# A decoder layer on one core: the order of the steps on VectorE, GpSimd and ScalarE is rewritten

## What is computed

```
# mixer
zxbcdt = u @ W_in;  z, xBC, dt = split(zxbcdt);  dt = softplus(dt + dt_bias)
xBC = silu(conv4(xBC) + conv_b);  x, Bm, Cm = split(xBC)
y = ssd(x * dt, -exp(A_log) * dt, Bm, Cm, chunk=64) + x * D_param
yf = y * silu(z);  out = (yf * rsqrt(mean(yf*yf) + 1e-5) * norm_w) @ W_out
# cross-attention
q = rmsnorm(h @ Wq + bq) * qn_w;  k = rmsnorm(ctx @ Wk + bk) * kn_w;  v = ctx @ Wv + bv
out = softmax(q @ k.T * 128**-0.5 + mask) @ v @ Wo
# feed-forward, qa = 8-bit rounding per token, qw = weights rounded to -1, 0, 1 times a scale
h = silu(qa(x) @ qw(w_gate).T) * (qa(x) @ qw(w_up).T)
out = qa(rmsnorm(h) * ln_weight) @ qw(w_down).T
# layer
x = x + mixer(layernorm(x));  x = x + xattn(layernorm(x), ctx);  x = x + ffn(layernorm(x))
```

## Time and profile before

| | |
|---|---|
| device time, median of 3 runs | 1235.27 us (1234.82 to 1237.11) |
| the profiled execution's own time | 1235.27 us |
| its span in the trace | 1233.2 us |
| PE busy | 1152.9 us, 93% |
| PEld busy | 991.5 us, 80% |
| DVE busy | 1004.4 us, 81% |
| POOL busy | 960.3 us, 78% |
| ACT busy | 735.7 us, 60% |
| DMA, mean over the span | 30 GB/s |
| mean granted TensorE clock | 0.973 |

### The profile page before, as it was taken

One profiled execution on the slowest core, in us unless ns is written; L12 is line 12 of the kernel. 1 busy time (PEld: TensorE's weight loads), 2 busy tenths in 40 slices (PEclk: granted clock), 3 DMA queues, 4 the chain that ended last, 5 costly groups with the idle time before them and its releaser, 6 DMA issues.

```text
span 1233.2 us, 34450 instructions
## 1 busy us (share of the span) xinstructions
PE 1152.9 (93%) x11539; PEld 991.5 (80%) x11571; DVE 1004.4 (81%) x2508; ACT 735.7 (60%) x1878; POOL 960.3 (78%) x1532
## 2 busy tenths in 40 slices
PE   3787999999999999999999999999999999999863
PEld 3676888988888889888888898888888888887742
DVE  3676888888898888888888888898888888988654
ACT  3665666555566765566666655566665556666521
POOL 3687888988888888888888888888889888877641
PEclk8798999999999999999999999999999999999977
DMA  8310011000000000000000000000000000011000
GB/s 282 88 48 10 6 28 28 26 26 21 21 8 26 26 26 26 21 26 18 12 26 26 26 26 21 26 13 17 26 26 26 26 21 25 6 23 23 14 13 26
DMA packets 64455, 37.04 MB, mean 30 GB/s; under 512 B 41504, under 2 KB 62752, under 8 KB 64160
## 3 DMA queue, kind: packets, MB, share of 16 engines
q1 hardware_dynamic: 61488, 36.50, 10.5%
q10 hardware_dynamic: 2928, 0.03, 0.1%
HBM read 23.93 MB, written 4.19 MB: 23 GB/s over the span
## 4 chain that ended last, share of the span: by engine, by line
PE 56%; DVE 17%; issue 11%; POOL 9%; ACT 4%; DMA 2%; DVEq 0%; POOLq 0%; ACTq 0%; SPq 0%
PE bank L1428 14%; PE bank L1319 5%; PE bank L1320 5%; PE bank L1321 5%; PE bank L1347 4%; PE bank L1488 4%; PE bank L1401 3%; PE bank L1356 3%; DVE xc L959 3%; PE bank L1336 2%; PE bank L1551 2%; PE bank L1510 2%; DVE hh L1116 2%; PE bank L1544 1%; DVE yT L1009 1%
## 5 line engine op out<-in xcount | busy, mean ns | idle before, releaser
L1428 PE MATMUL bank<-xcT,wq 128*128 128x128 f32 x2048 | 236.0, 276 | 1.6 <-ACT xcT L712 1.6
L1428 PEld LDWEIGHTS bank<-xcT,wq 128*128 128x128 f32 x2048 | 231.1, 192 | 5.9 <-issue 2.0
L959 DVE SCALAR_TENSOR_TENSOR xc<-bank,cw,xc 128x124 f32<-128x124 f32 (+2 forms) x576 | 163.5, 339 | 13.8 <-ACT xc L682 9.0
L456 POOL TENSOR_TENSOR rq<-rq,minus_half 128x16 f32<-128x16 f32 x32 | 93.9, 2934 | 91.8 <-DVE rq L1060 91.8
L1319 PE MATMUL bank<-wo_hi,o_hi 128*128 128x256 f32 x512 | 149.5, 292 | 0.0
L1320 PE MATMUL bank<-wo_lo,o_hi 128*128 128x256 f32 x512 | 144.0, 281 | 0.0
L1321 PE MATMUL bank<-wo_hi,o_lo 128*128 128x256 f32 x512 | 143.8, 281 | 0.0
L731 ACT ACTIVATE qT<-bank,bqT 128x128 f32<-128x128 f32 x384 | 109.9, 369 | 54.5 <-PE bank L1428 54.3
L468 POOL TENSOR_TENSOR pr<-pr,mask 128x512 f32<-128x512 f32 x64 | 80.0, 1271 | 24.4 <-DVE pr L1067 24.3
L1319 PEld LDWEIGHTS bank<-wo_hi,o_hi 128*128 128x128 f32 x512 | 97.0, 189 | 0.5 <-issue 0.4
L1320 PEld LDWEIGHTS bank<-wo_lo,o_hi 128*128 128x128 f32 x512 | 96.9, 189 | 0.1
(11 more groups left out here) (231 smaller groups left out, 3396.6 us busy)
## 6 DMA issues: line engine op xcount, KB each, us to landing
x_in<-in_x SPq DMA_DIRECT2D x32, 128.0 KB, 2.1
c_in<-in_ctx SPq DMA_DIRECT2D x32, 128.0 KB, 2.0
x_m<-in_x SPq DMA_DIRECT2D x32, 128.0 KB, 2.2
out<-x SPq DMA_DIRECT2D x32, 128.0 KB, 1.7
wq<-in_L_xattn_Wq SPq DMA_DIRECT2D x1, 2048.0 KB, 14.4
stage<-in_L_xattn_Wo SPq DMA_DIRECT2D x2, 1024.0 KB, 7.4
w_in<-in_L_attn_W_in SPq DMA_DIRECT2D x1, 1024.0 KB, 6.1
qT<-in_L_ffn_w_gate SPq DMA_DIRECT2D x1, 1024.0 KB, 10.2
```

The lines of the kernel that those rows point to most:

```text
L456: g.tensor_tensor(rq[:, 1, :], rq[:, 0, :], minus_half[:, :], ALU.pow).then_inc(s["x_rq"].sem, 1)
L959: last = v.scalar_tensor_tensor(out=o, in0=src, scalar=cw[:, j, TAPS - 1 - back:TAPS - back], in1=o, op0=ALU.mult, op1=ALU.add)
L1428: last = mm(x_Qbank[g][:, (n % 4) * P:(n % 4 + 1) * P], wq[:, c, n * HD:(n + 1) * HD], xcT[:, c, :], start=(c == 0), stop=(c == DC - 1))
```

## The change

No instruction is added or taken away in the steady bodies, and PE's order and SP's order stay as they are. Steps trade places in `body` on three engines:

- POOL: `m_norm` goes from before `m_skip` to behind the first `x_o_low`; `x_split` is followed by the first `x_o_low`, and `f_scales` stands behind `m_norm`; `x_khat` goes ahead of `x_rms` and `m_rms`.
- ACT: `x_q_bias(2)` goes ahead of `m_tanh_x`; the second `x_o_copy` ahead of `f_T_copy`; two of the `x_o_high` copies trade places; `f_keep` goes behind `m_tanh_bc`.
- DVE: `m_weights` goes to the front, `m_average` behind `f_range`, `m_xdt` ahead of `m_mix`, `m_norm` behind `m_gate`, one `x_o_low` ahead of `m_gate` and the other between the two feed-forward halves, `x_q_mean` behind `m_total`, and in the tail of the body the order is `f_weight`, `m_conv_bc`, `f_highest`, `m_residual`, `m_silu_z`, `x_vb_add`. `f_value` is merged into `f_gate`, with the same two instructions.

The diff, cut:

```diff
@@ POOL body
-                if ms is not None and first not in (0, 1):
-                    m_norm(ms)
                 if m is not None:
                     m_skip(m)
...
                 if xa is not None and first != 1:
                     x_split(xa)
+                if xb is not None:
+                    x_o_low(xb, 0)
...
-                if first in (0, 1):
+                if ms is not None:
                     m_norm(ms)
                 if f is not None:
                     f_scales(f)
                 if xb is not None:
-                    x_o_low(xb, 0)
                     x_o_low(xb, 1)
...
                 if xa is not None:
+                    x_khat(xa)
                     x_rms(xa)
                 if m is not None and first not in (0, 1):
                     m_rms(m)
-                if xa is not None:
-                    x_khat(xa)
@@ ACT body
                     x_exp(xb, 1)
+                if xa is not None:
+                    x_q_bias(xa, 2)
                 if m is not None:
                     m_tanh_x(m)
                 if xa is not None:
-                    x_q_bias(xa, 2)
                     x_q_bias(xa, 3)
...
                     x_o_high(xb, 1, 1)
-                    x_o_high(xb, 0, 1)
+                    x_o_high(xb, 1, 0)
+                    x_o_copy(xb, 1)
                 if f is not None:
                     f_T_copy(f)
@@ DVE body
+                if m is not None:
+                    m_weights(m)
                 if ms is not None and first not in (-1, 0, 1):
                     m_spread(ms)
...
                 if m is not None:
+                    m_xdt(m)
                     m_mix(m)
-                    m_xdt(m)
                 if f is not None:
                     f_quant(f)
...
-                if ms is not None and first not in (-1, 0, 1):
-                    m_norm(ms)
                 if m is not None:
                     m_skip(m)
...
+                if xb is not None:
+                    x_o_low(xb, 1, 0)
                 if m is not None:
                     m_gate(m)
...
+                if ms is not None and first != 0:
                     m_norm(ms)
...
+                if xa is not None:
+                    x_kv(xa)
+                if f is not None:
+                    f_gate(f, 0)
                 if xb is not None:
                     x_o_low(xb, 0, 1)
...
                 if f is not None:
                     f_gate(f, 1)
-                if xa is not None:
-                    x_q_mean(xa)
-                if f is not None:
-                    f_value(f, 1)
...
                 if f is not None:
                     f_weight(f)
+                if mn is not None:
+                    m_conv_bc(mn)
+                if f is not None:
+                    f_highest(f)
```

More of the change, by code:

```diff
@@ L217, in decoder_layer @@
           x_sum0+x_inv0+x_sum1+x_inv1 x_p0+x_p1 x_PT0+x_PT1 x_pT0+x_pT1 x_O0+x_O1
[L218 removed]
+          x_oh00+x_of00+x_oh11+x_oh10+x_of11+x_oh01 x_ol00+x_ol11 x_ol10+x_ol01 x_out x_x2
           f_copy f_stats+f_mean f_veps+f_rstd f_xn f_am+f_am2+f_r+f_s f_q1+f_q2 f_T f_qTc
@@ L829, in body @@
                     x_o_high(xb, 1, 1)
-                    x_o_high(xb, 0, 1)
+                    x_o_high(xb, 1, 0)
+                    x_o_copy(xb, 1)
                 if f is not None:
                     f_T_copy(f)
-                if xb is not None:
-                    x_o_copy(xb, 1)
                 if xa is not None:
@@ L844, in body @@
                 if xb is not None:
-                    x_o_high(xb, 1, 0)
+                    x_o_high(xb, 0, 1)
                 if xa is not None or m is not None:
@@ L864, in body @@
                     f_square(f)
-                    f_keep(f)
                 if mn is not None:
@@ L877, in body @@
                     w_turned(2)
+                if f is not None:
+                    f_keep(f)
                 if first == 1:
@@ L1177, in body @@
                 if xb is not None:
+                    x_max(xb, 0)
                     x_max(xb, 1)
@@ L1187, in body @@
                     f_residual(fb)
-                if ms is not None and first not in (-1, 0, 1):
-                    m_average(ms)
                 if m is not None:
-                    m_weights(m)
                     m_silu_x(m)
@@ L1195, in body @@
                     f_range(f)
+                if ms is not None and first not in (-1, 0, 1):
+                    m_average(ms)
                 if m is not None:
+                    m_xdt(m)
                     m_mix(m)
-                    m_xdt(m)
                 if f is not None:
@@ L1204, in body @@
                     m_spread(ms)
-                if first == -1:
-                    m_average(ms)
-                    m_norm(ms)
-                if ms is not None and first not in (-1, 0, 1):
-                    m_norm(ms)
                 if m is not None:
@@ L1213, in body @@
                     dve.wait_ge(s["p_olo"].sem, 2)
+                if xb is not None:
+                    x_o_low(xb, 1, 0)
                 if m is not None:
                     m_gate(m)
-                if first in (0, 1):
+                if first in (-1, 0, 1):
                     m_average(ms)
@@ L1222, in body @@
                     w_round(1)
+                if ms is not None and first != 0:
                     m_norm(ms)
+                if first == 1:
                     dve.wait_ge(s["w_attn"].sem, 16 * W_ATTN)
-                if xb is not None:
-                    x_o_low(xb, 0, 1)
                 if xa is not None:
@@ L1230, in body @@
                     f_gate(f, 0)
-                    f_value(f, 0)
                 if xb is not None:
-                    x_o_low(xb, 1, 0)
+                    x_o_low(xb, 0, 1)
                 if f is not None:
                     f_gate(f, 1)
-                if xa is not None:
-                    x_q_mean(xa)
-                if f is not None:
-                    f_value(f, 1)
                 if first == 0:
@@ L1250, in body @@
                     m_total(m)
+                if xa is not None:
+                    x_q_mean(xa)
                 if first == -1:
@@ L1254, in body @@
                     m_dt_ratio(mn)
-                if xa is not None:
-                    x_vb_add(xa)
                 if f is not None:
                     f_weight(f)
+                if mn is not None:
+                    m_conv_bc(mn)
+                if f is not None:
+                    f_highest(f)
                 if first == 0:
                     x_norm(m)
+                if first in (-1, 0, 1):
+                    m_silu_bc(mn)
                 if m is not None and first != 0:
@@ L1263, in body @@
                     x_stats(m)
-                if f is not None:
-                    f_highest(f)
-                if mn is not None and first not in (-1, 0, 1):
+                if mn is not None:
                     m_silu_z(mn)
[L1268 to L1272, removed]
+                if xa is not None:
+                    x_vb_add(xa)
                 if f is not None:
@@ L1276, in body @@
                     x_residual(xb)
+                if m is not None and first != 0:
+                    x_norm(m)
                 if mn is not None and first not in (-1, 0, 1):
                     m_silu_bc(mn)
-                if m is not None and first != 0:
-                    x_norm(m)
                 if xb is not None:
@@ L1516, in x_output @@
                     after(pe, x_ol[1][1], t + 1)
-                    after(pe, x_ol[1][0], t + 1)
+                    after(pe, x_ol[0][1], t + 1)
                 for n in range(half * NH // 2, (half + 1) * NH // 2):
```

3 lines of the change are left out of this document (removed).

## The result

The changed kernel takes 1254.84 us (median, 1254.27 to 1255.6) against 1235.31 us before, a ratio of 1.0155 (95% interval 1.0142 to 1.017). It is 19.5 us slower; the forecast was 1236.5 us, with a range up to 1247.

A forecast was written before the change was run, and what follows sets the result against it. The prediction took PE to bound the steady body, busy 35.22 of 35.40 us. From 1235.27 us, -3.1 (steady bodies), +4.0 (start) and +0.3 (end) gave 1236.5 us, range 1230.5 to 1247.

The forecast's parts named there:

- POOL's tail: Steady body's end: `x_khat` first, `f_weight` issued 0.15 us after L451; POOL ends no later, DVE regains the 0.8 it loses.
- `x_vb_add`: DVE, steady body: its move was said to cost nothing, covered by PE's 35.2 us of work, and gain nothing.
- Rival C: POOL becomes the bound: `f_weight` issued before L451, last probabilities reach PE 0.35 us late every body; 1249.4 us, chance 0.10.
- The gain at the value product: Steady body: DVE's value step and PE's value product come 0.15 us earlier, taken as 0.11 in 28 bodies, -3.1.
- rival E: Steady body: POOL's scale (L499) comes late, costing 0.31 us in each of 28 bodies; 1245.2 us, chance 0.09.
- rival F: Steady part unchanged: the norm or a scale 0.15 us late holds the gate product at 531.3; 1239.6 us, chance 0.09.
- its cover: Steady body: `f_qb` is issued at 527.2 to 527.5, 0.2 to 0.5 us ahead of POOL's `o_lo` at 527.68.
- rival D: `f_qb` falls behind POOL's `o_lo` in every body, PE's `f_transpose` 1.0 us late; 1267 us, chance 0.05.
- The start: Bodies 0 to 2: `mw`, swapped behind `xdt`, meets POOL's long steps; +1.45, +2.3 and +0.3, sum +4.0 us.
- The end: Bodies 31 and 32: `f_qb` escapes POOL's `o_lo`, -1.1; later `x_khat` chain, +1.4; together +0.3 us, between -1.1 and +1.5.
- the low end of the range: 1230.5 us: the start costing nothing, a steady gain of 0.15 us a body and the end's better bound.
- the swap of `m_xdt` and `m_mix` in the steady body: DVE, steady body: `m_xdt` before `m_mix` was said to cost nothing, covered by PE's work, and gain nothing.

The follow-up runs named there:

- run 5: The changed kernel with POOL's `m_rms` put between `x_khat` and `x_rms`: 1242.59 us, 1.0056 of the kernel before.
- run 2: The changed kernel with `x_vb_add` put back ahead of `f_weight` on DVE: 1.0058 of the kernel before.
- run 1: The changed kernel with POOL's tail in the old order `x_rms`, `m_rms`, `x_khat`: 1245.36 us, 1.0071 of the kernel before.
- run 10: As run 9, with POOL's `m_norm` ahead of its first `x_o_low` from body 2 on: 1.0184 of the kernel before.
- run 6: As run 5, with `m_mix` ahead of `m_xdt` in bodies 0 and 1 alone: 1240.49 us, 1.004 of the kernel before.
- run 11: The kernel before with `m_xdt` ahead of `m_mix` alone, in all bodies: 1235.58 us, 0.9996 of the kernel before.
- run 3: The changed kernel with `m_mix` ahead of `m_xdt` again on DVE, in all bodies: 1.0435 of the kernel before.
- run 9: The changed kernel with POOL's tail as before, `x_vb_add` ahead of `f_weight`, and `m_mix` first in bodies 0 and 1: 1236.18 us, 1.0003 of the kernel before.
- run 4: The kernel before with POOL's `x_khat` ahead of `x_rms` and `m_rms` alone: 1.0821 of the kernel before.
- run 7: As run 6, with `f_scales` ahead of POOL's first `x_o_low`: 1268.73 us, 1.0261 of the kernel before.

## Why the prediction was wrong

**The step that failed** is POOL's tail: "ends the body no later than before. DVE loses 0.8 there and has it back, because `m_residual` no longer leaves it idle". The prediction worked out when POOL's row ends and not when `m_rms` ends inside it. Three groups in another order end together at the same time, but the one that moves from second to third ends later by all of `x_khat` (0.28 + 1.12 + 1.04, and the held 0.9). The prediction's own times had it: with `x_rms` from 537.0 and 2.94 long, `m_rms` ends at about 540.8, 2 us behind the 538.85 of before. It measured 3.15, and what POOL does behind the row (`f_rms`) came 0.6 late as well. `m_residual` waits 1.96 us, where 0.95 stood and the prediction had nothing, and through `x_residual` it delays the second half of the scores. That place is neither of those that the prediction told to watch.

The delay reached PE with the help of a second step that the prediction counted at nothing, `x_vb_add`, now 0.60 us between `m_residual` and `x_residual`. Undoing the place of `m_rms` alone gives back 0.43 us a body (run 5), undoing that of `x_vb_add` alone 0.40 (run 2). These are not shares of a sum: PE lost 0.51 at the scores, and either is enough to take it away. By the same reckoning the 0.9 of the held L451 might be a third, but no run takes it alone out of the kernel after.

**Rival C** had the mechanism half right. Its condition came true (`f_weight` 0.17 ahead of L451; the forecast had 0.15 the other way), but its place (the probabilities, L1488 after) is wrong. With `m_rms` out of its way the lock is worth at most 0.16 of the body (run 5 against 1). What it is worth in the kernel after isn't shown: in run 2, with the order of those two restored, the same 0.9 us moved to L456.

**Right in kind.** The gain at the value product is 0.15 a body, as worked out, but just ahead of it PE gives up 0.12 at the mixer's sums (run 1: start of the sums' last part to the next 0.45 for 0.32). There ACT's tanh waits for L499, stretched to 0.53 by DVE's gate, and the square stands behind the tanh; in run 10, where L499 comes early, the two bodies that escaped have the 0.12 back. That is rivals E and F: the front, the swap included, is worth 0.03 a body. `f_qb` was never held (0.293 to 0.296 us in all 32), but its cover, put at 0.2 to 0.5 us, was 0.08: POOL's `o_lo` is issued at 536.90, and it is so in 24 of 25 full bodies. So it was luck as much as the forecast that kept rival D out.

The start cost 3.6 us for a forecast of 4.0, with a `mw` of 1.77 us in body 0 and 4.77 in body 1; run 6 shows that it hangs on the swap in bodies 0 and 1. PE stood idle for 5.30 us in front of body 1's mix, and from 66 to 72 us it then ran at 0.50 of full speed, where before 62 to 68 ran at 1.00 and 68 to 72 at 0.57.

The end cost 1.9 for 0.3; runs 1, 2 and 5 move it between 0 and +4.3 by the order of POOL's tail and the place of `x_vb_add`. `f_qb` did escape there (PE waits 2.6 us for it instead of 3.6), and PE waits 0.3 us at the turn of the keys instead of 2.8, but it waits 4.1 for `x_residual` in the last three bodies and did not before. The rest of the end isn't resolved. One bound was worked out wrongly: the low end of the range, by its own terms, is 1235.27 - 4.2 - 1.1 = 1230.0 and not 1230.5.

**Counted at nothing, and worth most**: the swap of `m_xdt` and `m_mix` in the steady body. It is worth 0.15 alone (run 11), and in the changed kernel it holds off 1.8 us a body (run 3).

The sum by its terms: forecast -3.1 + 4.0 + 0.3 = +1.2; measured +14.4 + 3.6 + 1.9 = +19.9.

What stays open: how the 0.16 of `x_khat` first divides between the held L451 and the later `f_rms`, for which DVE waits 1.09 in run 5 and 0.94 in run 1. All of it is lost where PE turns the mixer's x, the place at which the long bodies of run 9 lose theirs. The swaps on ACT were not undone one by one; run 9 shows only that all that is left together makes nothing.

## What to carry to other kernels

When steps trade places on one engine, write down the new end of each result and who reads it, not the end of the row: here the row as a whole ended 0.6 us later and one result in it 3 us later. Where two moves delay the same result, undo each alone, and don't add what they give back. Ask of each DVE step that reads SBUF alone which POOL step is running when it issues; a forecast margin under 0.2 us is to be read as either order, and priced at both. A change made of many swaps can hide a good one: this one's best part was a swap counted at nothing, and it was found by running it alone.

## What the runs showed of the hardware

- The hold goes by who starts first, but not with every step. POOL's L456 (128x16, a power) took 2.93 us in run 1 with the whole of DVE's 1.22 us `f_weight` inside it, and neither was longer. Issued behind `f_weight`, it took 3.89 (runs 2 and 4). The Trainium skill (SBUF, State Buffer; Who interferes with whom) gives the rule for both directions alike; here the second agrees, and the first does not.
- The held DVE step need not have two SBUF inputs. The norm (`tensor_scalar`, 128x256) stood 1.35 and 1.51 us behind POOL's `o_lo` in runs 7 and 10, and L1107 1.28 in run 3, against 0.41 and 0.34 alone. Steps with an input in PSUM were not held: `xdt` took 0.69 us in body 1 of run 11, issued at 60.68 inside a POOL step of 1.04 us (60.01), and `x_kv` 0.67, issued at 530.70 inside POOL's second `o_lo`.
- One and the same program falls on either side of such a race from body to body: 35.26 or 36.3 us in run 10, 36.1 or 37.8 in run 3, and 35.40 or 35.57 in run 9, where a small POOL step took 0.50 us in seven bodies, issued 0.02 to 0.03 us ahead of a DVE step with two SBUF inputs, and 0.20 to 0.22 in the others, issued 0.03 to 0.08 ahead.
